# Six stages of a decoder as three programs instead of six, with the mixers in half batches

## What is computed

```python
x = _layernorm(x + _L0_attn_ref(x, ...))      # 16 heads, causal softmax
x = _layernorm(x + _L0_xattn_ref(ctx, ctx, x, ssm_kernel, D, 8))   # long convolution of k*v, times q ("mixer one")
x = _layernorm(x + _L0_ffn_ref(x, W_g, W_u, W_d))                  # signs of the weights, quantised activations
x = _layernorm(x + _L1_attn_ref(x, W_in, ...))                     # state space, chunked scan
x = _layernorm(x + _L1_xattn_ref(x, k, bias, ctx, ctx, 8))         # the same convolution, x in k*v ("mixer two")
x = _layernorm(x + _L1_ffn_ref(x, w_gate, w_up, w_down))           # ternary weights, Hadamard transform
```

## Time and profile before

| | us |
|---|---|
| median of three runs | 851.48 |
| the profiled execution | 852.26 |
| its span, first to last instruction | 850.4 |
| attention | 0 to 184.97 |
| mixer one | 186.00 to 279.16 |
| feed-forward one | 279.88 to 409.00 |
| state space | 409.98 to 585.50 |
| mixer two | 586.48 to 680.84 |
| feed-forward two | 681.56 to 850.4 |

### The profile page before, as it was taken

One profiled execution on the slowest core, in us unless ns is written; L12 is line 12 of the kernel. 1 busy time (PEld: TensorE's weight loads), 2 busy tenths in 40 slices (PEclk: granted clock), 3 DMA queues, 4 the chain that ended last, 5 costly groups with the idle time before them and its releaser, 6 DMA issues. The chain is left out here.

```text
span 850.4 us, 13389 instructions
## 1 busy us (share of the span) xinstructions
PE 753.7 (89%) x4390; PEld 511.3 (60%) x4414; DVE 639.4 (75%) x1291; ACT 397.5 (47%) x640; POOL 479.8 (56%) x660
## 2 busy tenths in 40 slices
PE   6999999969999698899689999975999859999895
PEld 5777777734443375677367777763444326777674
DVE  4667777736999776574579999972799978988874
ACT  2555555652000245543287778851000025777785
POOL 1112333346774444341237777796677359899993
PEclk9999999989999799999699999987999969999998
DMA  7800000021000500000021221103000000000001
GB/s 262 350 2 2 1 2 2 2 77 72 1 0 0 189 2 1 1 1 2 3 99 54 71 76 51 50 1 109 6 0 0 1 2 1 1 14 20 13 20 38
DMA packets 12579, 33.96 MB, mean 40 GB/s; under 512 B 2656, under 2 KB 8032, under 8 KB 11232
## 3 DMA queue, kind: packets, MB, share of 16 engines
q1 hardware_dynamic: 12512, 33.11, 10.8%
HBM read 30.94 MB, written 2.16 MB: 39 GB/s over the span
## 5 line engine op out<-in xcount | busy, mean ns | idle before, releaser
L1058 PE MATMUL ss_b<-XT,win_late 128*128 128x256 f32 x320 | 88.8, 410 | 4.5 <-DVE ss_xc L1274 4.1
L466 POOL TENSOR_TENSOR at_kbd<-at_qk,at_hmask 128x512 f32<-128x512 f32 x16 | 16.7, 1041 | 111.6 <-DVE at_qk L393 111.6
L583 PE MATMUL m_y<-m_kv,toep 128*128 128x512 f32 x128 | 67.9, 612 | 10.6 <-POOL m_kv L572 10.6
L572 POOL TENSOR_TENSOR m_kv<-XT,CTXT 128x1024 f32<-128x1024 f32 x32 | 61.6, 1949 | 24.6 <-PE m_y L585 21.6
L603 DVE TENSOR_REDUCE MIX<-m_pr 128x128 f32<-128x1024 f32 x64 | 74.7, 1210 | 0.0
L572 POOL TENSOR_TENSOR m_kv<-CTXT 128x1024 f32<-128x1024 f32 x32 | 59.8, 1893 | 24.4 <-PE m_y L585 22.1
L1058 PEld LDWEIGHTS ss_b<-XT,win_late 128*128 128x128 f32 x320 | 59.0, 200 | 19.1 <-DVE ss_xc L1274 11.4
L1274 DVE SCALAR_TENSOR_TENSOR ss_xc<-ss_b,cw_late,ss_xc 128x254 f32<-128x254 f32 x144 | 66.6, 477 | 4.7 <-ACT ss_xc L1164 1.2
L584 PE MATMUL m_y<-m_kv,toep 128*128 128x512 f32 x128 | 67.1, 607 | 0.0
L585 PE MATMUL m_y<-m_kv,toep 128*128 128x512 f32 x128 | 66.4, 601 | 0.0
L1552 PE MATMUL f_b<-had_last,f_ht 128*128 128x256 f32 x256 | 61.8, 385 | 0.0
(11 more groups left out here) (233 smaller groups left out, 1934.2 us busy)
## 6 DMA issues: line engine op xcount, KB each, us to landing
MIX<-cum_rows SPq DMA_DIRECT2D x16, 512.0 KB, 3.7
toep<-toep_dram SPq DMA_DIRECT2D x2, 2048.0 KB, 12.7
X<-x_dram SPq DMA_DIRECT2D x1, 2048.0 KB, 12.7
MIX<-wgu_dram SPq DMA_DIRECT2D x1, 2048.0 KB, 7.9
CTXT<-ctxT_dram SPq DMA_DIRECT2D x1, 2048.0 KB, 18.3
ctx_last<-ctx_dram SPq DMA_DIRECT2D x1, 2048.0 KB, 8.8
out_dram<-f_o SPq DMA_DIRECT2D x16, 128.0 KB, 1.7
XT<-xT_dram SPq DMA_DIRECT2D x1, 1280.0 KB, 8.4
```

The costliest lines, as they stand in the source:

```text
L466: nc.gpsimd.tensor_tensor(KBD[n % 2][:, :, :, :], QK[n % 3][:, 2:4, :].unsqueeze(2).broadcast_to([P, 2, 2, S]), hmask[:, :].unsqueeze(1).u ...
L572: m = nc.gpsimd.tensor_tensor(KV[k][:, c, :, :].rearrange("p (b j) i -> p b j i", b=B), ki, vj, ALU.mult)
L583: nc.tensor.matmul(bY[k][0][h][:, :], toep[:, a, 0:P], kv[0], start=True, stop=True)
L1058: m = nc.tensor.matmul(bX[(NU * g + n) % 3][:, 0:GS_], win[:, h, off:off + P], XT[:, h, bass.ts(g, GS_)], start=(h == 0), stop=(h == C - 1))
```

## The change

1. Attention and mixer one become one program; so do feed-forward one, state space and mixer two. Feed-forward two stays apart. Six barriers become three.
2. The stages return step functions, and `interleave` alternates the steps of two stages on one engine. Mixer one's items begin behind attention's step 18, one item behind each step, on PE, DVE and POOL. The ten units of the state space's group 0 (with `taps`, `gate` and the silu) begin behind step 19 of feed-forward one; its front comes after them, in step 1, and `floor(0)`, `decay(0)`, `floor(1)` stand behind the taps of group 1. Mixer two's items begin behind the state space's step 8 on PE and DVE and behind its step 7 on POOL. PE, DVE and POOL do the items in this order; ACT does its mixer work after the steps of its first stage.
3. A mixer item is one head of half the batch: 32 items of two POOL products of 128x512, three PE products of 512 columns (six passes), two multiplications and one reduction (over both feature halves) on DVE. PSUM holds three items of two banks, POOL writes three buffers, and the reduction of item n stands behind the multiplications of item n+1.
4. Rounding the last stage's weights moves out of feed-forward one's loop into mixer one: ACT adds the constant and then takes `Sign` of the difference, so POOL's `clip` goes; the sum of magnitudes is formed behind PE item 24 and its inverse behind DVE item 25.
5. For that, weights and context lie in other buffers: the raw weights of feed-forward one in half of `MIX` and in `wgu1`, the context rows of the last stage in `wgu0` and `wd0`.

The core of the diff, without the indentation that moves:

```diff
+def interleave(first, n_first, second, n_second, start):
+    for i in range(max(n_first, start + n_second)):
+        if i < n_first:
+            first(i)
+        if i >= start:
+            second(i - start)
...
+HB, NI = B // 2, 2 * HM
-def mixer(ch, T, d, name, toep, skip):
+def mixer(ch, T, d, s, before, name, toep, skip, banks):
-    KV = [ch.sb(f"{name}_kv{k}", [P, C, B * J, J]) for k in range(2)]
+    KV = [ch.sb(f"{name}_kv{k}", [P, C, HB * J, J]) for k in range(3)]
+    bY = [banks[2 * k:2 * k + 2] for k in range(3)]
...
+    def gpsimd(pool):
+        def step(n):
+            h, a = divmod(n, HM)
+            if not skip and a == 0:
+                pool.wait_ge(before["x_kept"], HB * (h + 1))
+            upto(pool, s["conved"], n - 2)
...
+    def tensor(pe):
+        def step(n):
+            a = n % HM
+            if skip and n == 0:
+                pe.wait_ge(before["shifted"], 4 * B)
+            if skip and n == 2:
+                pe.wait_ge(before["back_kept"], B)
+                pe.wait_ge(before["ct_kept"], B)
...
+            pe.wait_ge(s["kv_made"], n + 1)
+            upto(pe, s["multed"], 2 * n - 4)
+            y, kv = bY[n % 3], [KV[n % 3][:, c, :, :] for c in range(C)]
+            nc.tensor.matmul(y[0][:, :], toep[:, a, 0:P], kv[0], start=True, stop=True)
+            nc.tensor.matmul(y[1][:, :], toep[:, a, P:2 * P], kv[0], start=True, stop=False)
+            nc.tensor.matmul(y[1][:, :], toep[:, a, 0:P], kv[1], start=False, stop=True).then_inc(s["conved"], 1)
...
+        def step(n):
+            times_q(n)
+            if n:
+                add_up(n - 1)
...
+            if n == NI - 1:
+                add_up(n)
...
+        for k in range(3):
+            nc.scalar.activation(staged[k], staged[k], ACT.Identity, scale=T["inv_w"][:, k:k + 1], bias=T["rnd"][:, :]).then_inc(s["rounded"], 1)
+        act.wait_ge(s["signed"], 2)
+        for k in range(3):
+            act.wait_ge(s["rounded"], k + 1)
+            dst = T["wd1"][:, :, :] if k == 2 else T["wgu1"][:, :, bass.ts(k, FF)]
+            nc.scalar.activation(dst, T[("wg1", "wu1", "wd1_raw")[k]][:, :, :], ACT.Sign, bias=T["unrnd"][:, :])
...
 def ffn0(...)
-                for k in range(3):
-                    if i == whole_at[k]:
-                        whole(k)
-                    if i == subtract_at[k]:
-                        subtract(k)
...
-                for k in range(3):
-                    if i == clip_at[k]:
-                        clip(k)
...
 def state_space(...)
             def unit(g, n):
+            if n == 0:
+                pe.wait_ge(before["x_kept"], GB * (g + 1))
+            if g == 0 and n < 3:
+                pe.wait_ge(before[("silu1_made", "p1_made", "p0_made")[n]], B)
...
+        def step(i):
+            if i == 1:
+                front()
...
+        def head(k):
+            unit(0, k)
+        return step, head
...
 def program(nc, d, out):
+            start, na = B + 2, B + 8
+                    interleave(at.tensor(pe), na, m0.tensor(pe), NI, start)
+                    interleave(at.vector(dve), na, m0.vector(dve), NI, start)
+                    interleave(at.gpsimd(pool), na, m0.gpsimd(pool), NI, start)
...
+                nf, n_head, n_space, heads_at, mix_at = B + 9, NU, NG + 5, B + 3, NG
+                        interleave(f0.tensor(pe), nf, head, n_head, heads_at)
+                        interleave(step_from(step, 1), n_space - 1, m1.tensor(pe), NI, mix_at - 1)
...
+                        interleave(st.gpsimd(pool), n_space, m1.gpsimd(pool), NI, mix_at - 1)
```

More of the change, by code:

```diff
@@ L44, in held, with run, step_from @@
     eng.sem_inc(passed, 1)
[L47 to L55, removed]
+Stage = namedtuple("Stage", "sync tensor scalar vector gpsimd")
+def interleave(first, n_first, second, n_second, start):
[4 more added lines that the diff above has]
+            second(i - start)
+def run(step, n):
+    for i in range(n):
+        step(i)
+def step_from(step, first):
+    return lambda i: step(first + i)
 class Chip:
@@ L1080, in scan @@
-            def scan(n):
-                if not 0 <= n < B:
-                    return
-                upto(pe, s["y1_made"], n)
-                pe.wait_ge(s["xdt_made"], n + 1)
-                pe.wait_ge(s["m_made"], n + 1)
-                for h in range(NH):
-                    o = HP * (h % 2)
-                    m = nc.tensor.matmul(bY[o:o + HP, bass.ts(h // 2, S)], XDT[n % 2][:, bass.ts(h, HP)], LA[n % 2][:, h, :], start=True, stop=True)
-                m.then_inc(s["y_made"], 1)
@@ new lines, in step @@
+        def step(i):
+            if i == 1:
+                front()
+            tap3(i, 0)
+            if i > 1:
+                floor(GB * (i - 1))
+            tap3(i, 1)
+            square(GB * (i - 2))
+            keep_x(GB * (i - 5))
+            tap3(i, 2)
+            if i > 1:
+                decay(GB * (i - 1))
+            tap3(i, 3)
+            keep_x(GB * (i - 5) + 1)
+            keep_xs(GB * (i - 1))
+            tap3(i, 4)
+            if i > 1:
+                floor(GB * (i - 1) + 1)
+            tap3(i, 5)
+            if i == 1:
+                floor(0)
+                decay(0)
+                floor(1)
+            keep_xs(GB * (i - 1) + 1)
+            decay(GB * (i - 1) + 1)
+            gate(i, 0)
+            square(GB * (i - 2) + 1)
+            gate(i, 1)
+            silu(i)
+            gate(i, 2)
+            gate(i, 3)
@@ L1238, in _, with head, vector, front @@
+        def head(k):
+            if k == 0:
+                act.wait_ge(before["later_in"], 160)
+            if k < CC:
+                tap3(0, k)
+            else:
+                gate(0, k - CC)
+                if k == CC + 1:
+                    silu(0)
+        return step, head
+    def vector(dve):
+        def front():
             dve.wait_ge(dt_made, 1)
@@ L1908, in phase, with tiles, done @@
+        def tiles(f, *a, side="left", keep=None):
+            ch.side = side
+            with ExitStack() as own:
+                ch.scope = own
+                made = f(ch, T, *a)
+                if keep is not None:
+                    keep.push(own.pop_all())
+            return made
+        def done():
             nc.clear_and_free_semaphores(ch.sems)
             nc.all_engine_barrier()
-        phase(attention)
-        with ExitStack() as late:
-            ch.scope = late
-            late_tiles(ch, T)
-            staging_tiles(ch, T)
-            phase(mixer, "m0", T["toep"], True)
-            phase(ffn0)
-            phase(state_space)
```

2851 lines of the change are left out of this document (1458 added, 1393 removed).

## The result

| | before | after |
|---|---|---|
| median of seven runs, us | 851.56 | 849.12 (846.92 to 851.04) |
| ratio, 95% interval | | 0.9961 [0.9949, 0.9973] |
| profiled execution, us | 852.26 | 846.92 |
| span, us | 850.4 | 845.1 |
| mean granted clock of PE | 0.955 | 0.958 |

Forecast were 840.7 us, 10.8 less than before. The gain is real and less than a third of that: 0.4%, about 3.3 us by the ratio. The step that failed is the border state space / mixer two: the forecast priced the first mixer items there at full clock, and PE ran them at half clock.

What follows compares the result with a forecast made beforehand. PE was taken to bound the mixer, with full stages and losses at the borders. 852.26 - 7.6 - 9.4 + 6.8 - 0.6 = 841.5 us, less 0.8 for the median: 840.7; case range 833 to 848, wider range 830 to 849.5.

Steps and rivals of the forecast that it cites:

- state space / mixer two: Border where mixer two's items interleave with the state space's last steps: gain 0.6 us, bounds gain 19.9 to loss 7.
- Attention / mixer one: Border where six mixer items lie between attention's last steps: gain 7.6 us, bounds a gain of 23 to a loss of 23.
- Feed-forward one: Stage that the last stage's rounding work leaves, ending waits on POOL: gain 9.4 us, bounds 7 and 10.5.
- Rival 3: Feed-forward one: rounding's cost was elsewhere, only 3 of 9 us won, 847 us; chance 0.12.
- Feed-forward one / state space: Border where group 0's units move into the drain, front behind them: loss 6.8 us, bounds 0 and 11.
- The median: Whole kernel: the median of runs is taken 0.8 us under the profiled execution, so 841.5 becomes 840.7.
- the range of 833 to 848: Whole kernel: own range in us of the forecast's case, which has chance 0.60.
- Rival 1: All three drains: items take only idle time, the clock stays full, 823 us; chance 0.12.
- Rival 2: Attention's drain: each interleaved item costs 9.4 us instead of 4.3; 871 us at the bound, 856 at half; chance 0.09.
- Rival 4: Sum of borders: front and mixer two's border at losses cancel the gains, 849.5 us, or 851; chance 0.07.
- the band: Whole kernel: what a measurement can tell from no change, about 0.2%, 1.7 us; chance of same 0.06.

Runs made afterwards that it cites:

- mixer one behind attention: Changed kernel with mixer one's items behind all attention steps on PE and DVE, POOL's products three items ahead: 847.96 us, ratio 0.9941.
- The clip experiment: Kernel before the change, without POOL's three clips of the last stage's weights, ACT's passes kept: 848.44 us, ratio 0.9946.
- with the gaps filled: Changed kernel with 4, 2 and 5 matmuls of 512 columns on PE ahead of the waits of mixer two's items 0, 1, 2: 841.57 us, ratio 0.9869.
- a shorter drain: Kernel with both mixers behind and front first, plus PE fillers before the state space's last five turns and the softplus wait: 827.16 us, ratio 0.9696.
- at the start: Kernel with both mixers behind and front first, plus ten 512-column matmuls on PE at the very start: 825.94 us, ratio 0.9694.

## Why the prediction was wrong, step by step

- **Attention / mixer one: right.** Forecast 271.6 and item 6 at 200.5; measured 270.95 and 200.04. The six items between the steps hid about what they cost; mixer one behind attention shows that the overlap itself is worth nothing there. One reading ahead of the sum was off: from 676.10 to 678.50 + 2.34 are 4.74 us and not 4.82, which is 2.48 + 2.34; no term rests on it.
- **Feed-forward one: right.** 8.9 of 9.4 us. Rival 3 (3 us) fell. The clip experiment adds that I had named POOL alone, and ACT had 2.6 of it. The 0.4 us for the operations on the weights' scale did not come: from mixer one's end to the first `add_down` it was 18.44 us and is 18.55.
- **Feed-forward one / state space: right in its chain, 2 us too dear.** The front started at 408.23; the chain gives 425.1 - 17.1 = 408.0. Its full-clock sum was 3.7, the measured loss 4.8; the 1 us lies in step 1 (20.43 us, forecast 19.4). I had added 3.1 for a clock between the two levels. The granted clock from 388 to 423 us was 0.79, within what I had named (0.6 to 0.8), but the stretch at half clock (0.50 from 396 to 404) fell where the units waited for the taps anyway and hardly moved the chain, and the front ran at full clock. That this term was 2 us too large hid a part of the next one's error: luck, not insight.
- **State space / mixer two: the step that failed.** Forecast a gain of 0.6, measured a loss of 6.0. I had PE's three waits (about 4, 4 and 2.5; measured 4.04, 4.64 and 2.59) and the queue behind them, but priced the items behind these waits at 2.57 us, the price of the full stage, and put half clock only into the bound, a loss of 7, near which the result lies. From `rstd(11)`'s end to the start of the last copy I counted 30.9 us; measured 37.8 (561.16 to 598.98), and with the gaps filled 31.6 (561.74 to 593.30). The order was right, the clock was not: it is 6.2 of the 6.6 us.
- **The median.** I carried over that an execution like the profiled one stands 0.8 over the median. After the change it stood 2.2 under it. That is 3.0 us, nearly as much as the whole gain, and without it the median would have lain inside the range of 833 to 848. Why it stood so low is not shown.
- **Rivals.** Rival 1 (the drains really fill) fell at all three borders. Rival 2 (lockstep) fell in attention, 4 us an item, but describes the state space's drain (25 us for four items), where I had not put it. Rival 4 gave the size (849.5) by sizes that did not come true: mixer two's border at a loss of 4 (measured 6.0) and the front at its bound of 11 (measured 4.8). Most of its chance was counted as no change, though 849.5 is 2.0 us under the median before and the band was 1.7.

## What to carry to other kernels

Work put between the last steps of a draining pipeline costs the queues that it passes its own length and the waits that it brings. At none of the three borders here did it pay, and at two it lost. Lay a stage behind the drain first, have the first operands ready from an engine that is idle, and interleave only what is then measured to win. Where a chain leaves TensorE standing, or with short turns only, price the matmuls behind it at half clock, in the sum and not in its bound: here that held behind waits of 4.04, 2.59 and 4.64 us, and for the first mixer item behind a row of short turns in three of four executions (first pair 2.04, 2.04, 1.76 and 1.10 us).

## What the runs showed of the hardware

- Eleven extra matmuls of 512 columns, in gaps that were there anyway, made the changed kernel 7.8 us faster (0.9869 against 0.9961). The same trick in a shorter drain and at the start won nothing (0.9696 and 0.9694 against 0.9698).
- The same group of 16 matmuls took 2.02 us in one execution and 3.75 in another, and the first mixer item behind the same short turns 2.65 and 4.27. A kernel's runs lie 2 to 5 us apart (846.92 to 851.04; 832.63 to 837.5), more than the 1.7 us of moving mixer one.
- The clock does not fall and rise at the gap's edges: behind a wait of 2.59 us the first pair took 1.10 us and the next 1.82.
